# The softplus chain of dt on GpSimd instead of VectorE, in the first stage of a selective-scan and expert layer

## The reference

```
xn      = channel layernorm of x
xz      = silu(in_proj(xn) + bias)              # 768 channels
x_ssm, res, gate = split(xz, 3)
xf      = silu(conv3_depthwise(x_ssm) + dw_b)   # 3 taps along the tokens
dbc     = dbc_w @ xf + dbc_b                    # per head and token: 1 value for dt, 8 for B, 8 for C
dt      = softplus(dbc[:, :, 0])
# tokens are permuted per head by an order computed from L0_conv_mobius; then the scan, per head:
h_t     = exp(dt_t * A) * h_(t-1) + (dt_t * B_t) * x_t ;   y_t = C_t . h_t + D * x_t
x       = x + silu(out_proj(unpermute(y) * silu(gate) + res) + bias)
t       = x + experts(token layernorm of x)     # 16 gated experts, then back to channels
```

## Time and profile before

| | us |
|---|---|
| median of 3 runs (1173.62 to 1174.06) | 1174.05 |
| the profiled execution's own time | 1165.49 |
| its span, first to last instruction | 1163.8 |
| PE busy | 989.5 (85%) |
| DVE busy | 861.0 (74%) |
| ACT busy | 505.7 (43%) |
| POOL busy | 457.4 (39%) |

### The profile page before, as it was taken

The page is one execution under the profiler, slowest core; times in us unless marked ns, Lnnn a source line. Parts: engine busy times, 40 slices in busy tenths (PEclk is TensorE's granted clock), DMA queues, the critical chain, the costliest instruction groups (busy, mean ns, idle before and its releaser), DMA issues.

```text
span 1163.8 us, 15111 instructions
## 1 busy us (share of the span) xinstructions
PE 989.5 (85%) x4482; PEld 736.6 (63%) x4482; DVE 861.0 (74%) x2121; ACT 505.7 (43%) x1034; POOL 457.4 (39%) x400
## 2 busy tenths in 40 slices
PE   4987799885377798898733999999999999999997
PEld 3876677675133454454422777777778777777776
DVE  5868766865288989889813688777788788877786
ACT  3655555554156656755612333332333333332331
POOL 2112212260358878878546433132233333142000
PEclk8998899898567766776766999999999999999999
DMA  6256533444513334343241303113041313122000
GB/s 184 110 121 179 139 91 119 137 118 118 139 32 106 99 101 108 90 115 92 66 155 37 134 32 120 50 64 114 18 144 36 144 34 127 40 72 106 0 19 37
DMA packets 77365, 108.97 MB, mean 94 GB/s; under 512 B 18394, under 2 KB 60676, under 8 KB 74244
## 3 DMA queue, kind: packets, MB, share of 16 engines
q1 hardware_dynamic: 70148, 90.37, 25.7%
q0 software_dynamic: 7168, 18.03, 5.4%
HBM read 60.46 MB, written 47.92 MB: 93 GB/s over the span
## 4 chain that ended last, share of the span: by engine, by line
PE 63%; DVE 12%; POOL 11%; issue 7%; DMA 3%; ACT 3%; ACTq 0%; SPq 0%; DVEq 0%; POOLq 0%
PE bank L1170 31%; PE bank L1051 5%; POOL stage L618 4%; PE bank L1086 4%; PE bank L949 4%; PE bank L1103 4%; PE bank L1054 3%; PE bank L1041 2%; PE bank L1012 2%; PE bank L1131 2%; PE bank L959 2%; POOL sp L554 1%; DMA score_scratch<-score 1%; POOL dtri L602 1%; POOL xtm L657 1%
## 5 line engine op out<-in xcount | busy, mean ns | idle before, releaser
L618 POOL TENSOR_TENSOR stage<-stage,rg 128x512 f32<-128x512 f32 x112 | 142.1, 1269 | 61.9 <-DVE rg L1594 52.3
L657 POOL DMA_INDIRECT xtm<-y_scratch,idxu x128 | 126.7, 990 | 83.3 <-issue 36.2
L1170 PE MATMUL bank<-wexph,xhl 128*128 128x512 f32 x512 | 144.8, 404 | 0.1
L669 POOL TENSOR_TENSOR ssm<-ssm,rg 128x512 f32<-128x512 f32 x32 | 37.5, 1196 | 270.3 <-DVE ssm L1674 270.3
L1170 PE MATMUL bank<-wexph,cr 128*128 128x512 f32 x512 | 141.7, 398 | 0.1
L1170 PEld LDWEIGHTS bank<-wexph,xhl 128*128 128x128 f32 x512 | 93.7, 189 | 23.4 <-DVE xf L1778 2.1
L785 ACT ACTIVATE rg<-dist,acol 128x256 f32<-128x256 f32 x256 | 108.2, 525 | 0.0
L1170 PEld LDWEIGHTS bank<-wexph,cr 128*128 128x128 f32 x512 | 93.2, 188 | 20.8 <-DVE ysb L1778 1.7
L1594 DVE TENSOR_TENSOR rg<-rg,bank 128x512 f32<-128x512 f32 x128 | 84.4, 680 | 27.3 <-PE bank L1041 21.5
L1170 PE MATMUL bank<-wexpl,xhl 128*128 128x512 f32 x256 | 80.9, 397 | 0.0
L1170 PE MATMUL bank<-wexpl,cr 128*128 128x512 f32 x256 | 79.2, 391 | 0.0
(11 more groups left out here) (289 smaller groups left out, 2131.9 us busy)
## 6 DMA issues: line engine op xcount, KB each, us to landing
xin<-in_x SPq DMA_DIRECT2D x16, 1024.0 KB, 5.6
res_gate_scratch<-rg SPq DMA_DIRECT2D x16, 1024.0 KB, 4.6
rg<-res_gate_scratch SPq DMA_DIRECT2D x8, 2048.0 KB
rows_scratch<-stage SPq DMA_DIRECT2D x8, 1160.0 KB, 9.0
y_scratch<-ysb SPq DMA_DIRECT2D x16, 512.0 KB, 3.8
out<-stage SPq DMA_DIRECT2D x16, 512.0 KB, 2.8
bc_scratch<-r SPq DMA_DIRECT2D x16, 288.0 KB, 3.0
bl<-bc_scratch SPq DMA_DIRECT2D x16, 192.0 KB
```

Source lines behind the costliest of these rows:

```text
L618: pool.tensor_tensor(ksum, dskip.rearrange("p t n -> p (t n)") if s == 0 else ksum, ee[:, s, :], ALU.add).then_inc(summed.sem, 1)
L657: pool.indirect_dma_start(out=xtm[:, t, h * P:(h + 1) * P], out_offset=None, in_=y_d.rearrange("q s r c -> (q s r) c"), in_offset=bass.Ind ...
L1170: last = pe.matmul(bank[4 + i][:, :], x_[:, k, i * P:(i + 1) * P], w[:, 2 * ep * KC + k:2 * ep * KC + k + KC + 1:KC, :], start=(n + k == 0 ...
```

## The change

In GpSimd's list `exp_rows` is replaced by `softplus_front` (the power, u+2, its reciprocal as a power of -1, the product, the square: 5 instructions, each waiting for the one before) and `softplus_back` (14 dependent instructions, then dt and dt*B into `stage`). Front and back of batch b-1 stand in batch b, on either side of `deviations(b+1)`; `low_experts` and both `scatter_order` come behind them. The scaled additions that VectorE did in one instruction are two on GpSimd. In VectorE's list `dbc_chain` is gone, and `dbc_in(b-1)` stands at the start of batch b, with the maximum of x and 0 in it and one more wait, for `rows_ready` of the batch before. The left out part of the diff counts one more set-up step in `pool_setup`.

```diff
--- before.py
+++ after.py
         rstd = sb("rstd", [P, NT])
+        minus = sb("minus", [P, HEADS * NT])
...
-        neg_ready = signal("neg_ready", 1)
-        exp_neg = signal("exp_neg", 1)
+        neg_ready = signal("neg_ready", 2)
...
+        soft_front = signal("soft_front", 5)
...
-        soft_steps = signal("soft_steps", 13)
+        soft_steps = signal("soft_steps", 14)
...
+            pool.memset(minus[:, :], -1.0).then_inc(pool_setup, 1)
...
-            def exp_rows(b):
-
-                pool.wait_ge(neg_ready.sem, neg_ready.at(b, 1))
-                pool.tensor_tensor(sp[:, 1, :], euler[:, :], sp[:, 0, :], ALU.pow).then_inc(exp_neg.sem, 1)
+            TERMS = 7
+
+            def softplus_front(b):
+
+                own = Steps(pool, soft_front, b)
+                pool.wait_ge(neg_ready.sem, neg_ready.at(b, 2))
+                own.did(pool.tensor_tensor(sp[:, 1, :], euler[:, :], sp[:, 0, :], ALU.pow))
+                own.settle()
+                own.did(pool.tensor_scalar(sp[:, 2, :], sp[:, 1, :], 2.0, None, ALU.add))
+                own.settle()
+                own.did(pool.tensor_tensor(sp[:, 2, :], sp[:, 2, :], minus[:, :], ALU.pow))
+                own.settle()
+                own.did(pool.tensor_tensor(sp[:, 2, :], sp[:, 2, :], sp[:, 1, :], ALU.mult))
+                own.settle()
+                own.did(pool.tensor_tensor(sp[:, 3, :], sp[:, 2, :], sp[:, 2, :], ALU.mult))
+                own.end()
+
+            def softplus_back(b):
+
+                own = Steps(pool, soft_steps, b)
+                pool.wait_ge(soft_front.sem, soft_front.at(b, 5))
+                own.did(pool.tensor_scalar(sp[:, 4, :], sp[:, 3, :], 1.0 / (2 * TERMS + 1), 1.0 / (2 * TERMS - 1),
+                                           ALU.mult, ALU.add))
+                own.settle()
+                for k in range(TERMS - 2, 0, -1):
+                    own.did(pool.tensor_tensor(sp[:, 4, :], sp[:, 4, :], sp[:, 3, :], ALU.mult))
+                    own.settle()
+                    own.did(pool.tensor_scalar(sp[:, 4, :], sp[:, 4, :], 1.0 / (2 * k + 1), None, ALU.add))
+                    own.settle()
+                own.did(pool.tensor_tensor(sp[:, 4, :], sp[:, 4, :], sp[:, 3, :], ALU.mult))
+                own.settle()
+                own.did(pool.tensor_scalar(sp[:, 4, :], sp[:, 4, :], 1.0, 2.0, ALU.add, ALU.mult))
+                own.settle()
+                own.did(pool.tensor_tensor(sp[:, 4, :], sp[:, 4, :], sp[:, 2, :], ALU.mult))
+                own.settle()
+                own.end()
+                rows = stage[:, :, :].rearrange("p t (h c) -> p (t h) c", h=HEADS)
+                pool.tensor_tensor(rows[:, :, P], sp[:, 4, :], sp[:, 5, :], ALU.add).then_inc(rows_ready.sem, 1)
+                pool.wait_ge(rows_ready.sem, rows_ready.at(b, 1))
+                pool.tensor_tensor(rows[:, :, P + 1:P + 1 + S], dbx[:, :, 1:1 + S], bc(rows[:, :, P], 2, S),
+                                   ALU.mult).then_inc(rows_ready.sem, 1)
 
             def low_experts(j):
...
             for b in range(NB):
+                if b:
+                    softplus_front(b - 1)
                 if b + 1 < NB:
                     deviations(b + 1)
+                if b:
+                    softplus_back(b - 1)
+                if 1 <= b <= WEXP_PARTS:
+                    low_experts(b - 1)
+                if b == NB - 3:
+                    scatter_order(0)
                 if b == NB - 2:
                     scatter_order(1)
-                if 1 <= b <= WEXP_PARTS:
-                    low_experts(b - 1)
-                exp_rows(b)
-                if b == NB - 3:
-                    scatter_order(0)
+            softplus_front(NB - 1)
+            softplus_back(NB - 1)
...
                 dve.wait_ge(dbc_full.sem, dbc_full.at(b, 1))
                 dve.wait_ge(rows_stored.sem, rows_stored.at(b, 0))
+                dve.wait_ge(rows_ready.sem, rows_ready.at(b, 0))
                 rows = bank[D_BANK][:, 0:NT * HEADS * R].rearrange("p (t h r) -> p t h r", h=HEADS, r=R)
                 dve.tensor_tensor(dbx[:, :, :].rearrange("p (t h) r -> p t h r", h=HEADS), rows[:, :, :, 0:1 + S],
                                   bc(dbcb[:, :, 0:1 + S], 1, NT), ALU.add).then_inc(dbc_used.sem, 1)
@@ -1399,37 +1444,7 @@
                 dve.wait_ge(dbc_used.sem, dbc_used.at(b, 2))
                 dve.scalar_tensor_tensor(sp[:, 0, :], dbx[:, :, 0], -1.0, dbx[:, :, 0], ALU.mult, ALU.min).then_inc(
                     neg_ready.sem, 1)
-
-            TERMS = 7
-
-            def dbc_chain(b):
-
-                own1 = Steps(dve, soft_steps, b)
-                own1.did(dve.tensor_scalar(sp[:, 5, :], dbx[:, :, 0], 0.0, None, ALU.max))
-                dve.wait_ge(exp_neg.sem, exp_neg.at(b, 1))
-                own1.did(dve.tensor_scalar(sp[:, 2, :], sp[:, 1, :], 2.0, None, ALU.add))
-                own1.settle()
-                own1.did(dve.reciprocal(sp[:, 2, :], sp[:, 2, :]))
-                own1.settle()
-                own1.did(dve.tensor_tensor(sp[:, 2, :], sp[:, 2, :], sp[:, 1, :], ALU.mult))
-                own1.settle()
-                own1.did(dve.tensor_tensor(sp[:, 3, :], sp[:, 2, :], sp[:, 2, :], ALU.mult))
-                own1.settle()
-                own1.did(dve.tensor_scalar(sp[:, 4, :], sp[:, 3, :], 1.0 / (2 * TERMS + 1), None, ALU.mult))
-                own1.settle()
-                for k in range(TERMS - 1, 0, -1):
-                    own1.did(dve.scalar_tensor_tensor(sp[:, 4, :], sp[:, 4, :], 1.0 / (2 * k + 1), sp[:, 3, :],
-                                                      ALU.add, ALU.mult))
-                    own1.settle()
-                own1.did(dve.scalar_tensor_tensor(sp[:, 4, :], sp[:, 4, :], 1.0, sp[:, 2, :], ALU.add, ALU.mult))
-                own1.settle()
-                rows = stage[:, :, :].rearrange("p t (h c) -> p (t h) c", h=HEADS)
-                dve.scalar_tensor_tensor(rows[:, :, P], sp[:, 4, :], 2.0, sp[:, 5, :], ALU.mult, ALU.add).then_inc(
-                    rows_ready.sem, 1)
-                dve.wait_ge(rows_ready.sem, rows_ready.at(b, 1))
-                dve.tensor_tensor(rows[:, :, P + 1:P + 1 + S], dbx[:, :, 1:1 + S], bc(rows[:, :, P], 2, S),
-                                  ALU.mult).then_inc(rows_ready.sem, 1)
-                own1.end()
+                dve.tensor_scalar(sp[:, 5, :], dbx[:, :, 0], 0.0, None, ALU.max).then_inc(neg_ready.sem, 1)
 
...
                 if b:
-                    dbc_chain(b - 1)
+                    dbc_in(b - 1)
                 convolve(b, 0)
...
-                dbc_in(b)
...
             for b in range(NB):
                 batch(b)
+            dbc_in(NB - 1)
             for i in range(2):
                 dve.wait_ge(mm_full[i].sem, mm_full[i].at(NB, 0))
             for v in cr:
                 dve.memset(v.bitcast(F32), 0.0).then_inc(cr_zero, 1)
             dve.wait_ge(wexp_low, WEXP_PARTS)
             dve.memset(hs[0][0:SUB, :], 0.0).then_inc(cr_zero, 1)
-            dbc_chain(NB - 1)
```

More of the change, by code:

```diff
@@ L515, in _ @@
             pool.iota(token[:, :, :], [[HEADS, NT], [1, HEADS]], base=0, channel_multiplier=NT * HEADS).then_inc(pool_setup, 1)
-            pool.wait_ge(pool_setup, 6)
+            pool.wait_ge(pool_setup, 7)
             pool.affine_select(out=ident[:, :], in_=ident[:, :], compare_op=ALU.not_equal, fill=1.0, base=0,
@@ L531, in _ @@
             deviations(0)
-            pool.wait_ge(pool_setup, 15)
+            pool.wait_ge(pool_setup, 16)
             pool.affine_select(out=cumu[:, :], in_=cumu[:, :], compare_op=ALU.is_ge, fill=0.0, base=0,
@@ L537, in _ @@
                                    pattern=[[-1, P]], channel_multiplier=1).then_inc(pool_setup, 1)
-            pool.wait_ge(pool_setup, 18)
+            pool.wait_ge(pool_setup, 19)
             pool.memset(same[0:SUB, 0:SUB], 1.0).then_inc(pool_setup, 1)
-            pool.wait_ge(pool_setup, 19)
+            pool.wait_ge(pool_setup, 20)
             pool.memset(same[SUB:P, SUB:P], 1.0).then_inc(pool_setup, 1)
-            pool.wait_ge(pool_setup, 20)
+            pool.wait_ge(pool_setup, 21)
             pool.affine_select(out=cumu[:, SUB:P], in_=cumu[:, SUB:P], compare_op=ALU.is_ge, fill=0.0,
@@ L983, in batch @@
                 rows_by_tokens(b)
-            pe.wait_ge(pool_setup, 7)
+            pe.wait_ge(pool_setup, 8)
             x_by_tokens(0)
@@ L1281, in constants @@
                                           ALU.subtract))
-                dve.wait_ge(pool_setup, 22)
+                dve.wait_ge(pool_setup, 23)
                 dve.wait_ge(act_setup, 2)
```

## The result

Four runs of the changed kernel took 1185.70 to 1187.82 us, median 1187.74; four of the kernel before 1172.11 to 1174.06, median 1173.84. The ratio is 1.0118, 95% interval 1.0100 to 1.0135: 13.9 us slower, where 9.4 were forecast (1183.5 us). On a second chip it was 1.0109 [1.0080, 1.0138]: 1176.75 against 1165.73, 11.0 us.

A forecast was written before the change was run, and what follows sets the result against it. No single engine bounded the first stage: GpSimd's power, VectorE's chain, convolutions, matmuls. At most 55 us go, but a loop over the rows' landing moves the last store 9.4 us later: 1183.5 us (1178 to 1190, chance 0.48; range 1167 to 1198).

The forecast's parts named there:

- c: The moment VectorE starts `convolve(b, 0)` in a batch; forecast 57.9 in batch 1, 103.8 in batch 2.
- Gone from VectorE's list: VectorE loses the wait for the power and 14 short instructions, 3.0 us; at most 55 us over seven batches.
- Prices on GpSimd: Durations of small dependent GpSimd steps: two-input 0.33 us, one-input 0.25, powers 2.9; front 7.0, back 4.8.
- Hindrance: Back's small GpSimd steps wait for VectorE instructions: 1.1 us for the first, 1.1 for the others; rows complete at c + 16.3.
- Batches 3 to 5: Front stands behind `low_experts` on GpSimd: rstd at c + 12.0 instead of 9.3, back ends at c + 18.1.
- The restart: From start of `stage_rows` to c: 4.9 us, 5.6 with `low_experts` in the way; TensorE's clock changes nothing.
- Landing: The store of rows lands 9.5 us after issue, taken as between median and longest.
- Score row: In batch 1 the score row, behind the store in SP's list, comes 12.0 us later; VectorE gets it at 99.6.
- The scatter: `scatter_order(0)`'s eight DMAs on GpSimd, to 236.5, hold front(5) until 244.2; rstd comes at 245.9.
- the first (no hindrance, 11 us faster): Small GpSimd steps slip between VectorE's instructions, rows at c + 14.2: 11.4 us earlier, 1162.6; chance 0.18.
- the point of decision: The no-hindrance case decides if GpSimd's back ends before about c + 15.3.
- Rival 4: A GpSimd power shuts VectorE out, the convolution starts 2.5 us later in seven batches: 17 more, 1201; chance 0.05.

The follow-up runs named there:

- the filler: Changed kernel with forty unused transposes on TensorE at the end of each batch, while it waits for staging: 1178.21 us, 1.0088 of the kernel before.
- the repetition: The unaltered changed kernel run and profiled again on a second chip: 1176.75 us against 1165.73 for the kernel before, 1.0109.
- With three terms: Changed kernel with 3 softplus polynomial terms instead of 7, 8 instructions fewer in each back: 1158.01 us, 0.9911 of the kernel before.
- the power first above: Kernel before with only `exp_rows` moved ahead of `low_experts` on GpSimd: 1160.77 us, 0.9962 of the kernel before.

## Why the prediction was right, step by step

The mechanism was the one forecast, and its numbers for c came within 2 us: batches 2 to 6 were predicted at 103.8, 135.3, 168.6, 201.9 and 233.4 and came at 101.90, 135.91, 169.93, 201.75 and 234.57; the last store at 298.7, against 300.92 here and 298.86 on the second chip. The time is 13.9 us longer, not 9.4: 11.6 are in the first stage, and the other 2.3 are within the interval (11.7 to 15.8). Part of the nearness is luck. In batch 3 three terms were off, the rows 2.6 us too late, the landing 1.4 and the restart 2.0 too short (33.3 predicted, 34.0 measured). And the batches were off one by one: from c of batch 2 on they were predicted at 31.5, 33.3, 33.3 and 31.5 and took 34.0, 34.0, 31.8 and 32.8.

- **Gone from VectorE's list**: right. c of batch 1 is 57.00 (57.9 predicted), and no wait for the power is left.
- **Prices on GpSimd**: a two-input step of 16 columns takes 0.31 us from start to start (0.33 taken), a one-input step 0.33 (0.25 taken), the power of -1 2.93 (2.9 taken). The back by itself, in the last batch, took 5.1 us instead of 4.8.
- **Hindrance**: right for the first step (L574, 1.12 us, begun under L1430), wrong for the others, for which I took 1.1 in all: beside the normalisation (L1405) they kept to 0.22 to 0.28. The rows are there at c + 15.5, not 16.3. I had put the normalisation with L1380 by its form. What a step waits for is seen in the last batch, where the front of the one before ran beside both convolutions; GpSimd, then VectorE:

```profile
267.73 1.27 POOL L565 TENSOR_TENSOR sp<-sp 128x16 f32<-128x16 f32 x1
269.08 1.23 POOL L567 TENSOR_TENSOR sp<-sp 128x16 f32<-128x16 f32 x1
...
271.11 1.26 POOL L578 TENSOR_TENSOR sp<-sp 128x16 f32<-128x16 f32 x1
```

```profile
267.63 1.28 DVE L1427 SCALAR_TENSOR_TENSOR xf<-ssm,dww,xf 128x1024 f32<-128x1024 f32 x1
268.95 1.28 DVE L1430 SCALAR_TENSOR_TENSOR xf<-ssm,dww,xf 128x1024 f32<-128x1024 f32 x1
...
271.00 1.29 DVE L1427 SCALAR_TENSOR_TENSOR xf<-ssm,dww,xf 128x1024 f32<-128x1024 f32 x1
```

  Each step of 0.22 us ends 0.1 us after the convolution's instruction that it lies under. The Trainium skill ("SBUF — State Buffer", section "Who interferes with whom") says that a VectorE instruction with two inputs in SBUF contends with a GpSimd instruction that reads SBUF; these rows agree.
- **Batches 3 to 5**: rstd was to come 2.7 us late, at c + 12.0, and the back to end at c + 18.1. They came at c + 9.3 and c + 15.5. The front did start behind `low_experts`, but 1.8 us ahead of c (168.11), since c itself was 2.0 us later than predicted relative to the landing: here one error hid another.
- **The restart**: this is the step that failed most plainly. I took 5.6 us from the arrival of the rows to c, measured in a kernel where TensorE had not been idle, and wrote that its clock changes nothing as long as the loop decides. The opposite holds: only when the loop decides is TensorE idle, and the restart took 6.5 to 7.8 us at 0.56 to 0.74 of the clock. With the clock at 1.00 it took 5.0 to 5.7 where the filler was not in the way, about what I had taken.
- **Landing**: 9.5 to 11.0 us in the batches, 10.1 in the mean, last store aside. The 9.5 taken were the lowest, not the middle.
- **Score row**: 10.2 us later, not 12.0, since the store came at c + 15.6 and c at 57.0. Its arrival released VectorE at 97.85 (99.6 predicted), and c of batch 2 came 4.1 us after it (4.2 taken).
- **The scatter**: predicted to hold front(5) until rstd was late. The front began at 234.56, 2 us earlier than predicted, and was through when the statistics were (241.7), at c + 7.2: it cost nothing. In the repetition, where c of batch 6 came at 231.79, it did: rstd was there at c + 12.3, VectorE waited 1.7 us for it, and the store left at c + 17.5. The last batch, from `dbc_in(7)` at 287.91 to the store, took 13.0 us (12.8 predicted).

Of the rivals, the first (no hindrance, 11 us faster) was wrong though half of its condition came true. It would have needed rows at c + 14.2. With three terms they are complete 2.5 us earlier, at c + 13.0, and that kernel is indeed faster than before; the runs put the point of decision, for which I wrote "about c + 15.3", between that and c + 15.5, and no closer. Rival 4, a power that shuts VectorE out, found no support: L1424 took its 0.81 and L1427 began at 170.78 and took its 1.28, both inside the power of L559 (168.11 to 171.04). It is GpSimd's 1024-column instruction that holds VectorE, as with the power first above.

## What to carry to other kernels

That an engine idles is no reason to move a dependent chain to it: ask first what the chain's last result starts, and who waits for that. Here it is a store whose landing frees the only buffer, so 3 us of relief on VectorE were paid with rows that are complete 15.5 us after c instead of before it; with a second buffer the move is worth 3.9 us a batch, and with the score's transfers ahead of the store as well the kernel takes 0.9745 of the kernel before. And where a wait moves to TensorE, price its restart at the clock that it gets after standing idle, here 0.56 to 0.74, not at the one of a kernel in which it doesn't stop there.

## What was not expected of the hardware

- After 5.3 us without work TensorE restarted at 0.58 of its clock, after 4.1 us at 0.74, after 3.9 us at 0.56, after 1.45 us (three terms) at 0.68, and with transposes in the gap at 1.00: the length of the stop alone doesn't tell the clock.
- GpSimd steps of 0.22 us last until the end of a 128x1024 three-operand instruction on VectorE (up to 1.27), and are not touched by its 128x256 subtract-and-multiply (L1405).
- GpSimd's 128x1024 two-input instruction (2.38 us) makes a VectorE step of 16 columns last 2.33 us instead of 0.17 and a 128x1024 one up to 2.57 instead of 0.81, while a power of 16 columns (2.93 us) lets VectorE's 128x1024 instructions through.
- A power of 16 columns with exponent -1 costs GpSimd the same 2.93 us as one with other exponents, and 3.90 where it began under a convolution.
